# Convolution chain on one core: the second stage's steps in a new order, the third convolution three steps behind the first

## The reference

```
x = x + _L0_conv_ref(_gn(x), 5)          # Newton-Schulz inverse, five steps per 128x128 matrix
x = x + _L1_conv_ref(_gn(x), ...)        # 3x3 convolution of the input quantised to 8 bits
x = x + _L2_conv_ref(_gn(x), filter_w)   # 5 taps along the diagonal, zero padding
x = x + _L3_conv_ref(_gn(x), weight)     # 3x3 convolution, circular (written with FFTs)
```

## Time and profile before

| | us |
|---|---|
| median of 3 runs | 4458.1 (4455.18 to 4465.2) |
| the profiled execution | 4457.7 |
| its span, first to last instruction | 4455.8 |
| second stage: `first` of image 0 to that of image 63 | 2285.7 to 4354.3 |
| PE busy | 4048.0 (91%) |
| granted TensorE clock, mean | 0.955 |

### The profile page before, as it was taken

The page is one execution under the profiler, slowest core; times in us unless marked ns, Lnnn a source line. Parts: engine busy times, 40 slices in busy tenths (PEclk is TensorE's granted clock), DMA queues, the critical chain, the costliest instruction groups (busy, mean ns, idle before and its releaser), DMA issues.

```text
span 4455.8 us, 91385 instructions
## 1 busy us (share of the span) xinstructions
PE 4048.0 (91%) x35017; PEld 3008.5 (68%) x35017; DVE 3169.5 (71%) x7333; ACT 2465.2 (55%) x4490; POOL 2416.8 (54%) x3154
## 2 busy tenths in 40 slices
PE   7999999999999999999958888888888888888887
PEld 7999999999999999999933333333333333333333
DVE  6888888888888888888855566656656666666563
ACT  6766767777777767777634344344444443444442
POOL 6888888888888888888732222222222222222221
PEclk9999999999999999999978999999999999999998
DMA  2211122212121122112135556555655665566553
GB/s 74 60 58 58 58 68 66 59 58 67 58 68 58 58 68 66 59 58 67 39 78 127 127 134 138 134 128 135 138 129 134 136 138 131 129 137 138 129 134 87
DMA packets 339921, 422.14 MB, mean 95 GB/s; under 512 B 25312, under 2 KB 288160, under 8 KB 323104
## 3 DMA queue, kind: packets, MB, share of 16 engines
q1 hardware_dynamic: 311840, 342.85, 31.8%
q10 hardware_dynamic: 27648, 73.43, 6.6%
HBM read 135.18 MB, written 134.22 MB: 60 GB/s over the span
## 4 chain that ended last, share of the span: by engine, by line
ACT 16%; POOL 12%; ACTq 10%; DVE 7%; issue 2%; PE 2%; DMA 1%; POOLq 0%
POOL xn L1228 12%; ACTq L1171 6%; ACT F L1276 6%; ACT xn L1279 5%; ACTq L1250 4%; ACT T L1269 3%; DVE xn L1327 2%; DVE T L1325 2%; DMA xk<-xn 1%; PE bank L1493 1%; DVE nb L1400 1%; PE bank L1498 1%; ACT xn L1262 1%; DVE r L1398 0%; DVE rb L1392 0%
## 5 line engine op out<-in xcount | busy, mean ns | idle before, releaser
L1228 POOL TENSOR_TENSOR xn<-F,xn 128x512 f16<-128x512 f32 x512 | 541.6, 1090 | 1608.0 <-ACT xn L1279 1608.0
L1493 PE MATMUL bank<-xk,wt 128*32 128x512 f16 x6144 | 717.2, 441 | 260.9 <-DMA xk<-xn 260.9
L1469 PE MATMUL bank<-xn,wt 128*128 128x512 f16 (+1 forms) x3072 | 784.1, 387 | 26.1 <-DVE xn L1327 14.4
L484 ACT ACTIVATE P<-bank 128x512 f32<-128x512 f32 x1024 | 606.2, 607 | 266.3 <-PE bank L1007 155.4
L1345 DVE SCALAR_TENSOR_TENSOR x<-bank,wu,x 128x512 f32<-128x512 f32 x512 | 381.7, 745 | 479.0 <-PE bank L1476 299.4
L1493 PEld LDWEIGHTS bank<-xk,wt 128*32 128x32 f16 x6144 | 280.2, 102 | 467.2 <-DMA xk<-xn 292.9
L1469 PEld LDWEIGHTS bank<-xn,wt 128*128 128x128 f16 (+1 forms) x3072 | 297.6, 101 | 394.2 <-issue 61.4
L1498 PE MATMUL bank<-xk,wth 128*32 128x512 f16 x3072 | 530.8, 425 | 0.0
L1276 ACT ACTIVATE F<-x,nb,r 128x2048 f32<-128x2048 f32 x128 | 268.0, 2094 | 306.0 <-DVE nb L1400 306.0
L334 POOL TENSOR_TENSOR W<-W 128x512 f16<-128x512 f32 x256 | 289.7, 1164 | 145.2 <-ACT W L517 145.2
L1356 DVE BATCH_NORM_STATS2 bs<-x 128x6 f32<-128x512 f32 x512 | 355.6, 695 | 17.6
(11 more groups left out here) (145 smaller groups left out, 8514.4 us busy)
## 6 DMA issues: line engine op xcount, KB each, us to landing
X<-in_x SPq DMA_DIRECT2D x64, 1024.0 KB, 4.9
x_scratch<-X SPq DMA_DIRECT2D x64, 1024.0 KB, 5.5
X<-x_scratch SPq DMA_DIRECT2D x64, 1024.0 KB, 8.7
out<-x SPq DMA_DIRECT2D x64, 1024.0 KB, 7.4
xk<-xn SPq DMA_DIRECT2D x256, 131.8 KB, 5.5
xk<-xn ACTq DMA_DIRECT2D x256, 131.8 KB, 5.8
xh<-xn SPq DMA_DIRECT2D x192, 131.8 KB, 4.4
xh<-xn ACTq DMA_DIRECT2D x192, 131.8 KB, 5.4
```

What stands on the lines that cost most here:

```text
L484: nc.scalar.activation(into[:, 4 * q:4 * q + 4, :], banks[q][:, :].rearrange("p (m w) -> p m w", m=4), ACT.Copy).then_inc(sb, 1)
L1228: ins = nc.gpsimd.tensor_tensor(padded(xn[l][odd], 1)[:, a + 1:a + 5, L:L + H], F[l][:, a:a + 4, :], padded(xn[l][odd], 0)[:, a + 1:a + 5, ...
L1469: nc.tensor.matmul(bank, wt[l][:, a, k, :], v, start=(k == a == b == 0), stop=False)
L1493: nc.tensor.matmul(bank[32 * q:32 * q + 32, :], wt[2][:, a, e, 32 * q:32 * q + 32], rows(b, 2 * q + e, 0), start=(a == b == e == 0), stop= ...
```

## The change

The second stage's order is laid anew on every engine. A step s now does convolution 1 of s, then convolution 3 of s-3, then convolution 2 of s-1, so there are B+3 steps where there were B+2. `xs[3]` gets a third buffer, with `out_stored` in three semaphores. The banks are now dealt out in the order of use (`order`, `place`), and `bank_free` waits for the chunk six places earlier in it.

```
-            xs = [None, x1s] + [[sb(f"x{l}_{n}", [H, NJ, H]) for n in range(2)] for l in (2, 3)]
+            THIRD = 3
+            xs = [None, x1s] + [[sb(f"x{l}_{n}", [H, NJ, H]) for n in range(k)] for l, k in ((2, 2), (3, THIRD))]
...
+            LATE = (None, 0, 1, 3)
+            STEPS = B + LATE[3]
...
+            order = [(l, s - LATE[l], u) for s in range(STEPS) for l in (1, 3, 2) if there(s - LATE[l]) for u in range(BPI)]
```

ACT's step after the change (s counts as before):

```
+                    for s in range(STEPS):
+                        if there(s - 1):
+                            act.wait_ge(normed[2], s)
+                            for r in range(1, RB, 2):
+                                skew_row(act, r, s - 1)
+                        if there(s + 1):
+                            quotients(s + 1)
                         if there(s - 2):
+                            root(3, s - 2)
+                            upper(3, s - 2)
                         if there(s + 1):
+                            first(s + 1)
                         if there(s):
                             root(2, s)
+                            upper(2, s)
+                        if there(s - 2):
+                            wrap(s - 2)
+                            act.wait_ge(wrapped, 2 * (s - 1))
+                            halo_copies(act, 3, s - 2, True)
```

SP: skew of s-1, load of s+2, halos of layer 1 of s+1, store of s-3, halos of layer 3 of s-2. POOL: lower of layer 3 of s-2, then of layer 2 of s. PE's and DVE's steps:

```
+                    for s in range(STEPS):
                         if there(s):
                             for u in range(BPI):
+                                conv(1, s, u)
+                        if there(s - 2):
+                            mean(3, s - 2)
+                        for u in range(BPI):
+                            if there(s - 3):
+                                conv(3, s - 3, u)
+                            if there(s - 2) and u == 0:
+                                var(3, s - 2)
+                            if there(s):
+                                if u == 1:
+                                    mean(2, s)
+                                if u == 3:
+                                    var(2, s)
                         if there(s - 1):
                             for u in range(BPI):
+                                diagonals(s - 1, u)
```

```
+                    for s in range(STEPS):
+                        for u in range(BPI):
+                            if u == BPI - 1 and there(s - 2):
+                                deviations(3, s - 2)
+                            if there(s):
+                                residual(1, s, u)
+                                chunk_stats(2, s, u)
                         if there(s):
                             whole_stats(2, s)
+                        if there(s - 2):
+                            variance(3, s - 2)
+                        if there(s + 1):
+                            quantise(s + 1)
+                        if there(s - 2):
+                            normalise(3, s - 2)
                         for u in range(BPI):
+                            if there(s - 3):
+                                residual(3, s - 3, u)
                             if there(s):
                                 if u == 0:
                                     deviations(2, s)
+                                if u == 2:
                                     variance(2, s)
+                                if u == 3:
+                                    normalise(2, s)
+                        for u in range(BPI):
+                            if there(s - 1):
+                                residual(2, s - 1, u)
+                                chunk_stats(3, s - 1, u)
                         if there(s - 1):
                             whole_stats(3, s - 1)
```

More of the change, by code:

```diff
@@ L1132, in conv_net @@
             high = [None, None] + [sem(f"high{l}") for l in (2, 3)]
[L1133 removed]
+            out_stored = [sem(f"out_stored{n}") for n in range(THIRD)]
             q_chain = sem("q_chain")
@@ L1177, in _ @@
                 def _(sp):
[L1178 to L1195, removed]
@@ L1217, in _, with load, store @@
-                    run(sp, step)
-                    for n in range(2):
-                        sp.wait_ge(out_stored[n], 16 * (B // 2))
+                    def load(n):
+                        stand(sp, evac[1], BPI * (n - 1), w_loaded, 16 * W_PIECES)
+                        sp.dma_start(xs_of(1, n)[:, :, :],
+                                     x1d[n, :, :, 0:H].rearrange("j p w -> p j w")).then_inc(x1_in[n % 2], 16)
+                    def store(n):
+                        sp.wait_ge(evac[3], BPI * (n + 1))
+                        sp.dma_start(out[n, :, :, :], xs_of(3, n)[:, :, :]).then_inc(out_stored[n % THIRD], 16)
@@ L1240, in _ @@
                     for n in range(2):
                         nc.gpsimd.memset(xk[n][:, :, :], 0.0).then_inc(xk_zeroed, 1)
-                    run(pool, step)
+                    for s in range(STEPS):
+                        if there(s - 2):
+                            lower(3, s - 2)
+                        if there(s):
+                            lower(2, s)
                 @block.scalar
                 def _(act):
[L1246 to L1251, removed]
@@ L1304, in step @@
[L1304 to L1313, removed]
@@ L1315, in _, with quantise @@
-                    quotients(0, 0, 0)
-                    first(0, 0, 0)
-                    run(act, step)
+                            upper(2, s)
[3 more added lines that the diff above has]
+                            halo_copies(act, 3, s - 2, True)
                 @block.vector
                 def _(dve):
-                    def quantise(n, h, odd):
+                    def quantise(n):
@@ L1438, in _ @@
-                    quantise(0, 0, 0)
-                    run(dve, step)
                 @block.tensor
                 def _(pe):
-                    def bank_free(s, l, u):
-                        k = BPI * (l - 1) + u - B_RING
-                        while True:
-                            if k < 0:
-                                k, s = k + 3 * BPI, s - 1
-                            if not isinstance(s, int) or s < 0 or there(s - k // BPI):
-                                break
-                            k -= B_RING
-                        need(pe, evac[k // BPI + 1], BPI * (s - k // BPI) + k % BPI + 1)
```

215 lines of the change are left out of this document (86 added, 129 removed).

## The result

| | before | after |
|---|---|---|
| median, us | 4458.65 (4455.18 to 4465.2, 4 runs) | 4185.77 (4182.59 to 4189.16, 4 runs) |
| span of the profiled execution | 4455.8 | 4187.4 |
| starts of `first`, image 0 and 63 | 2285.7, 4354.3 | 2286.5, 4081.4 |
| mean clock | 0.955 | 0.971 |

What follows compares the result with a forecast made beforehand. PE's wait for the skewed copies was taken as the bound, then ACT's cycle with DVE at 26.4 us per step: 2285.7 + 65 + 60 x 26.4 (1584) + 97 + 1.9 gives 4034 us, range 4008 to 4124.

Steps and rivals of the forecast that it cites:

- What bounded the kernel before: PE's long wait per step for the skewed copies xk, 4.2 us, with about 1.9 of slow clock after it.
- What would be late next: After the change, no longer PE's wait for one transfer but the longest of several cycles, ACT's, at 26.4 us per step.
- the ring of ACT and DVE (chain B): ACT's copy issues, quotients, quantise and the norms of layers 3 and 2, closing within one step: 26.3 us.
- three close cycles: Per step: PE's own work 25.4 us, PE's two-step chain through the halos 25.8, ACT with DVE 26.3.
- 1.46 for root and `normalise` of layer 2: Term of the ACT and DVE cycle, from root to F of layer 2: 1.46 us.
- halo issues 3.41, skew issues 4.30: Terms of the ACT and DVE cycle: three halo and four skew copy issues in a row on ACT, in us.
- the rival of the copies in each other's way: Fourteen copies in a row slow halo landing or ACT's issues: one us more per step, 4094 us, far end 4160; chance 0.27.
- ACT's halo and skew issues well above 3.4 and 4.3 us: Sign in the profile after that the forecast is wrong: ACT's copy issues take longer than those times.
- the end after the last `first`: From image 63's `first` to the span's end: last step, norms, halos, last chunks and store, 97 us.
- The halos' landing: From ACT's first halo issue to the matmul using them in convolution 3: 7.0 us; well above was a sign of being wrong.
- The clock rival: PE drops to its lower clock after short waits of 1.0 us per step: 4088 us; chance 0.05.
- The third x3 buffer costs nothing: The added xs[3] buffer costs no engine time; the store is issued near t0 + 17, its buffer written two steps later.

Runs made afterwards that it cites:

- experiment 1: Changed kernel with normalise's three two-column tensor_tensor products made tensor_scalar, the second column as the scalar: 4111.42 us.
- experiment 6: Kernel of experiment 1 plus four more small instructions in normalise of layer 2, writing a spare column: 4164.22 us.
- Experiment 2: Changed kernel with ACT's quotients ahead of its four skew issues: 4146.42 us.
- experiment 3: Changed kernel with PE doing var of layer 3 ahead of the halo wait in convolution 3's first chunk: 4176.67 us.
- experiment 10: Kernel of experiment 1 with PE doing both bodies of convolution 3 first and var of layer 3 behind them, quotients still behind the skew issues: 4116.23 us.
- experiment 4: Changed kernel with two x3 buffers instead of three: 4182.06 us.
- experiment 9: Kernel of experiment 7, but PE does var of layer 3 after the second body instead of after the first: 3989.91 us.
- experiment 5: Changed kernel with the edits of experiment 1, Experiment 2 and experiment 3 together: 4067.48 us.
- experiment 7: Kernel of experiment 5, but PE does the bodies of chunks 0 and 1 of convolution 3 before it waits for the halos: 4031.99 us.

## Why the prediction was wrong, point by point

**What bounded the kernel before: right.** The wait for xk is gone, and PE's work didn't change. Of the slow clock only half went: PE was busy 28.0 us per step before (682.12/800 of 32.8) and is 26.4 now (731.66/800 of 28.84), against 25.4 of work at full clock.

**What would be late next: right.** The prediction named the ring of ACT and DVE (chain B) as the longest of three close cycles. Experiments 1 and 6 show that a ring through `normalise` of layer 2 rules. Experiment 2, which opens only the ring of ACT and DVE, gains 39 us, and experiments 3 and 10, which take var from behind the halos, gain 9 and nothing: so it is the ring of ACT and DVE that rules in most steps, not the halos or PE.

**The sizes of its terms: wrong, and this is nearly the whole miss.** Means over some 50 steady steps of each kernel, worked out from the starts in the timelines:

| from start to start, us | forecast | after | experiment 1 |
|---|---|---|---|
| quotients to quantise | 2.12 | 2.21 | 2.20 |
| quantise to F of layer 3 | 3.67 | 3.61 | 3.78 |
| F of layer 3 to `first` | 4.03 | 4.14 | 4.16 |
| `first` to root of layer 2 | 2.00 | 2.03 | 1.95 |
| root to F of layer 2 | 1.46 | **2.89** | 1.63 |
| F of layer 2 to wrap | 4.04 | 3.94 | 3.95 |
| wrap to halo issue | 1.29 | 1.28 | 1.29 |
| halo issue over skew issue to quotients | 7.71 | **8.74** | 8.70 |
| sum | 26.3 | 28.8 | 27.7 |

Two terms failed. "1.46 for root and `normalise` of layer 2" is the first, +1.43 us. It was read from a row at which POOL was idle, while in the new order POOL's `lower` of layer 3 starts 4 us after F of layer 3, just when `first` starts, and runs for 4.2 us, so that it is still at work when layer 2's `normalise` comes 2 us later. I had laid out both in time and only asked whether POOL is late, not who works beside it. The trace of the kernel before had the sign of it, once, in a step that was a little late, with POOL's subtractions from 2504.33 on:

```profile
2504.99 0.45 DVE L1372 TENSOR_TENSOR dv<-dv 128x8 f32<-128x8 f32 x1
2505.48 1.01 DVE L1374 SCALAR_TENSOR_TENSOR dv<-bs,dv 128x8 f32<-128x8 f32 x1
```

Their usual times are 0.17 each. The Trainium skill, in "SBUF — State Buffer", section "Who interferes with whom", says that a DVE instruction with two SBUF inputs contends with a GpSimd instruction that reads SBUF. The rows above and experiment 1 agree: products with one input and a scalar take 0.21 us beside POOL.

The second is the issue time, "halo issues 3.41, skew issues 4.30", +1.03. The halos' part measured 3.43, so all of it is in the skew issues, 5.32 up to the quotients instead of 4.30. The lower end of the rival of the copies in each other's way came to the same sum ("0.15 to 0.3 more" for each of seven, and 7 x 0.15 is 1.05), though in truth it is four issues that are 0.25 slower. It had a chance of 0.27 but should have been in the forecast: seven issues in a row were the one thing of which the trace had no row, and I took them at the price of single groups. "ACT's halo and skew issues well above 3.4 and 4.3 us" was named as a sign of being wrong, and for the skew issues it came.

The sum closes: 60 steps x (28.84 - 26.4) = 146 us, and the end after the last `first` is 106.0 (4187.4 - 4081.4) instead of 97, another 9, whose cause stays open (the terms given for it, 10, 25, 39, 7.0 and 15, add up to 96). Together 155, against 155.7 between the forecast span (4031.7) and the measured one (4187.4). The start was right: image 3's `first` was forecast at 2350.7 and came at 2350.78.

**The halos' landing**, 7.0 from issue to use, was read from the last image, which has no skew copies behind it. In the changed kernel it is 8.5 to 8.7 in most steps, about 10 in some and 8.8 in the mean, and for its last image, again without skew copies, 7.0 (issue at 4164.02, use at 4170.99). It is another sign of being wrong that the prediction had named:

```profile
3026.92 2.13 PE L1444 MATMUL bank<-xn,wt 128*128 128x512 f16 x9
3033.79 1.46 PE L1449 MATMUL bank<-xh,wth 96*128 96x512 f16 x3 [4.74 <-DMA xh<-xn]
...
3035.33 4.00 PE L1444 MATMUL bank<-xn,wt 128*128 128x512 f16 x9
```

Nine matmuls take 4.00 us instead of 2.13 behind the wait of 4.74, so PE is at the lower clock there. The trace has such a stretch in 24 of the 52 steps from 2500 to 4000 us, each behind a wait for the halos of 2.7 to 4.8 us. In the changed kernel the two are worth at most the 9 us of experiment 3. In experiment 2 the landing is a term of the ring that rules.

**The clock rival** was too cheap at 0.05: the forecast was 0.99, and it is 0.96 in the second stage. But the lower clock is seen behind longer waits than 1 us, as told above, and in most steps it did not set the step (experiments 3 and 10).

**A third chain was missed.** Var of layer 3 stands behind the first chunk of convolution 3, and so behind the halo wait, and quantise behind variance. That makes a ring within one step that I didn't list. It costs 9 us in the changed kernel (experiment 3), and is what limits experiment 2.

**"The third x3 buffer costs nothing"**: right, and it gives nothing either (experiment 4).

**The range** reached to a step of 27.9, and 28.8 came. It allowed for 1.5 us more in the ring, which either of the two lengthened terms alone would have kept within, but not both.

## What to carry to other kernels

When a reorder takes the long wait off the busiest engine, write down every ring that is then close to the step's length, and for each of its terms ask what the neighbours do at that moment, not only how long the term was in the old trace. If several rings lie within a few per cent, the forecast should lean above the longest, since one mis-sized term in any of them lengthens the step and a gain in one of them doesn't shorten it. And once the ruling ring is known, an edit elsewhere gives nothing (experiment 10), while most of the same edit gave 77 us after the ring was opened (experiment 9 against 5): open first, then polish.

## What the runs showed of the hardware

- A DVE product of two SBUF columns of 128x1 takes 0.16 us alone. If it starts beside POOL's subtraction of 128x512 it ends when that instruction does, and so takes 0.80 (L1376) and 1.01 us (L1378) in the mean. With the second column as scalar it takes 0.21, beside POOL or not. `RECIPROCAL`, `BATCH_NORM_STATS2` (0.69) and the residual that reads a PSUM bank and one SBUF tile (0.75) are the same with or without POOL.
- Four DMA issues of 131.8 KB by ACT cost 3.73 us well behind other copies, 4.29 beside SP's four, and 5.21 beside SP's four and right behind the six halo copies (means). An engine that issues copies here pays for those in flight.
- With waits of 0.93 us per step on PE the clock was 0.99 (experiments 5 and 7); one of 4.74 us was followed by a stretch at the lower of the two levels.
